# Deformable convolution in two layers: weights of two output rows side by side for the contraction

## The reference

```
value = (xf @ vp_w.T + vp_b).reshape(n, L, G, cg)           # 8 groups of 8 channels
om_in = depthwise3x3(x, dw_w) + dw_b
om    = om_in @ om_w.T + om_b                               # per pixel, group: 9 taps x (dy, dx, mask)
py, px = row + dy_tap + off_y,  col + dx_tap + off_x
sampled = bilinear gather of value at (py, px), 0 outside   # 4 neighbours
out = einsum('nhwgk,nhwgkc->nhwgc', mask, sampled) @ op_w.T
x = x + out
```

## Time and profile before

| | |
|---|---|
| median of 3 runs | 2954.0 us (2952.28 to 2957.7) |
| span of the profiled execution | 2952.3 us (its own time is not given apart) |
| TensorE, matmuls | 2707.7 us busy, 92% |
| TensorE, weight loads | 2151.1 us, 73% |
| VectorE | 2190.7 us, 74% |
| ScalarE | 2106.7 us, 71% |
| GpSimd | 1925.4 us, 65% |
| line 1273 (contraction) | 20480 matmuls, 1033.8 us busy |
| mean granted clock | 0.971 |

### The profile page before, as it was taken

One profiled execution on the slowest core, in us unless ns is written; L12 is line 12 of the kernel. 1 busy time (PEld: TensorE's weight loads), 2 busy tenths in 40 slices (PEclk: granted clock), 3 DMA queues, 4 the chain that ended last, 5 costly groups with the idle time before them and its releaser, 6 DMA issues. The chain is left out here.

```text
span 2952.3 us, 99348 instructions
## 1 busy us (share of the span) xinstructions
PE 2707.7 (92%) x40456; PEld 2151.1 (73%) x40456; DVE 2190.7 (74%) x3095; ACT 2106.7 (71%) x4273; POOL 1925.4 (65%) x1451
## 2 busy tenths in 40 slices
PE   3999789993899999999999999999999999999998
PEld 2666456772677778787778777777878787777886
DVE  3555423334989898988889797989798888989763
ACT  2444256653887878787878787787878787878782
POOL 1000000003888988888888888888988888888892
PEclk8999889996899999999999999999999999999999
DMA  4555579974677777777777786777777777777675
GB/s 106 129 127 151 131 203 265 266 192 155 163 188 198 204 202 196 191 214 194 206 194 205 186 216 186 197 204 191 208 192 214 187 205 191 205 192 213 170 182 153
DMA packets 343610, 559.00 MB, mean 189 GB/s; under 512 B 159184, under 2 KB 245712, under 8 KB 342992
## 3 DMA queue, kind: packets, MB, share of 16 engines
q1 hardware_dynamic: 284112, 461.96, 62.0%
q10 hardware_dynamic: 59136, 91.76, 8.8%
HBM read 351.36 MB, written 202.19 MB: 187 GB/s over the span
## 5 line engine op out<-in xcount | busy, mean ns | idle before, releaser
L1273 PE MATMUL acc_p<-abuf,vbd 128*32 128x170 f32 (+9 forms) x20480 | 1033.8, 371 | 10.4 <-issue 9.6
L1273 PEld LDWEIGHTS acc_p<-abuf,vbd 128*32 128x32 f32 (+1 forms) x20480 | 805.1, 144 | 230.6 <-issue 24.9
L1106 ACT ACTIVATE dwt<-xp,wts 128x224 f32<-128x224 f32 x2016 | 803.3, 487 | 41.0 <-ACT wst L1130 32.3
L977 DVE TENSOR_TENSOR pr<-mh_p,ht 128x864 f32<-128x864 f32 x672 | 668.9, 1051 | 23.2
L1250 PE MATMUL win_p<-pr,smat 128*128 128x160 f32 x4032 | 617.0, 308 | 13.2 <-POOL pr L1063 12.2
L243 PE MATMUL cv<-cin,wb 128*64 128x392 bf16 x6912 | 590.1, 333 | 26.0 <-ACT cin L222 26.0
L1250 PEld LDWEIGHTS win_p<-pr,smat 128*128 128x128 f32 x4032 | 562.6, 192 | 39.1 <-issue 13.7
L243 PEld LDWEIGHTS cv<-cin,wb 128*64 128x64 bf16 x6912 | 401.7, 110 | 208.3 <-ACT cin L222 26.1
L1046 POOL TENSOR_TENSOR dwt<-dwt 128x896 f32<-128x896 f32 x224 | 519.1, 2317 | 4.7 <-ACT dwt L1106 4.7
L1060 POOL TENSOR_TENSOR pr<-pr 128x576 f32<-128x576 f32 x224 | 316.6, 1413 | 211.4 <-DVE pr L977 211.4
L967 DVE TENSOR_TENSOR mh_p<-oms,ht 128x864 f32<-128x864 f32 x224 | 392.3, 1752 | 7.1 <-ACT ht L1121 7.1
(11 more groups left out here) (131 smaller groups left out, 2579.7 us busy)
## 6 DMA issues: line engine op xcount, KB each, us to landing
abuf<-weight_scratch SPq DMA_DIRECT2D x784, 240.0 KB, 4.1
weight_scratch<-wst ACTq DMA_DIRECT2D x112, 800.0 KB, 5.1
xt<-x SPq DMA_DIRECT2D x128, 392.0 KB, 7.5
rows_scratch<-vsb SPq DMA_DIRECT2D x224, 128.0 KB, 3.2
vbd<-rows_scratch SPq DMA_DIRECT2D x896, 32.0 KB, 4.5
x_scratch<-xt SPq DMA_DIRECT2D x64, 392.0 KB, 6.7
y<-x SPq DMA_DIRECT2D x64, 392.0 KB, 5.4
x3h<-x_scratch SPq DMA_DIRECT2D x64, 392.0 KB, 5.7
```

The lines of the kernel that those rows point to most:

```text
L977: dve.tensor_tensor(pr[:, j % 2, slots, :, :, :].rearrange("p k e x z -> p e k (x z)"), mh[:, a, :, :].rearrange("p (k x) z -> p k (x z)", ...
L1106: ins = act.activation(dwt[:, j % 2, k, :].rearrange("p (r w) -> p r w", w=W), image[:, r:r + BR, k % 3:k % 3 + W], ACT.Identity, scale=dw ...
L1273: mm = pe.matmul(acc_p[32 * (2 * s + b):32 * (2 * s + b) + 32, 0:2 * TN].rearrange("p (k w) -> p k w", w=W)[:, k0:k1 + 1, x0:x1], vbd[0:K, ...
```

## The change

The weights of two neighbouring output rows (0 and 1, 2 and 3, ...) for one value row now stand next to each other. A value row that is at distance m from the first of them is at m - 1 from the second, so the odd rows' weights are stored one distance later. That makes six distances a pixel instead of five (`RP`), 96 values instead of 80; the two places that no weight falls into stay zero (`wst` is cleared once). The order within a pixel is now distance, group, row.

The contraction reads pairs of rows, `[1, 2]` innermost, and a value row takes part for up to three pairs. The sums stand in `acc_p` as column, row of the pair, and `copy_acc` sorts them out. `copy_weights` takes four instructions, one for each row of the tile; `win_p` is laid out with 172 columns a window column for that. `copy_om` sorts the groups so that the four groups of a lane set stay together. The clamp in `hats` writes into `ht[:, u, 0]`, which the last hat then overwrites, after a wait. The bands are read back in groups of eight pixels as before, 288 KB a read.

```diff
-PC = 2 * BR * RT * 2
+RP = RT + 1
+WP = 172
+PC = 2 * BR * RP * 2
 BAND = CT * PC
-LINE = GS * 12 * PC + PC
-SEEN = 12 * PC
+PX = 8
+SEEN = (PX + CT - 1) * PC
+LINE = GS * SEEN + PC
...
-        hj = sb("hj", [LANES, 2 * TAPS, BR * G])
...
-        READS = (4, 3)
+        READS = (32 // PX, 24 // PX)
...
-                    for b in range(4 * half, 4 * half + READS[half]):
-                        m = b % 4
-                        seen = bass.AP(lines.tensor, lines.offset + 8 * b * LINE, [[SEEN, 32], [XL * LINE, S], [1, SEEN]])
-                        at = (QB * half + 8 * m) * PC
-                        sp.dma_start(abuf[32 * m:32 * m + 32, :, at:at + SEEN], seen).then_inc(a_in[half], 16)
+                    for m in range(READS[half]):
+                        seen = bass.AP(lines.tensor, lines.offset + (32 * half + PX * m) * LINE,
+                                       [[SEEN, GS * PX], [XL * LINE, S], [1, SEEN]])
+                        at = (QB * half + PX * m) * PC
+                        sp.dma_start(abuf[GS * PX * m:GS * PX * (m + 1), :, at:at + SEEN], seen).then_inc(a_in[half], 16)
...
-                        oms[:, j % 2, :, :].rearrange("q w (k g) -> q w k g", g=G),
-                        om_p[:, :].rearrange("q (k z) -> q k z", k=BR)[:, :, 0:OMC].rearrange("q k (w g) -> q w k g", g=G),
-                        ombt[:, :].rearrange("q (w g) -> q w g", g=G).unsqueeze(2).broadcast_to([LANES, 3 * TAPS, BR, G]),
+                        oms[:, j % 2, :, :].rearrange("q w (b k g) -> q (w b) k g", b=2, g=GS),
+                        om_p[:, :].rearrange("q (k z) -> q k z", k=BR)[:, :, 0:OMC].rearrange("q k (v g) -> q v k g", g=GS),
+                        ombt[:, :].rearrange("q (v g) -> q v g", g=GS).unsqueeze(2).broadcast_to([LANES, 6 * TAPS, BR, GS]),
...
+                pool.memset(wst[:, :, :], 0.0)
...
-                    act.activation(hj[:, :, :], ht[:, u, 1, :, :], ACT.Relu, bias=minus1[:, :], accum_out=far[:, bass.ts(t, 1)])
+                    act.activation(ht[:, u, 0, :, :], ht[:, u, 1, :, :], ACT.Relu, bias=minus1[:, :], accum_out=far[:, bass.ts(t, 1)]).then_inc(far_ok, 1)
                     act.activation(ht[:, u, 1, :, :], ht[:, u, 1, :, :], ACT.Identity, scale=-1.0, bias=1.0)
+                    act.wait_ge(far_ok, t + 1)
                     act.activation(ht[:, u, 0, :, :], off, ACT.Relu, scale=-1.0).then_inc(hat_ok, 1)
...
-                    for h, cells in ((0, 3), (1, 2)):
-                        m, at = RT * cells, BANK * h
+                    for k in range(BR):
+                        to = 2 * BR * (2 - 2 * (k % 2)) + BR * u + k
+                        cells = wst[:, 0, to:to + 1]
                         ins = act.activation(
-                            wst[:, :, :].rearrange("p g (m v q) -> p v m g q", v=2, q=2 * BR)[:, u, 3 * RT * h:3 * RT * h + m, :, :],
-                            win_p[:, at:at + m * BR * G].rearrange("p (m q g) -> p m g q", m=m, g=GS), ACT.Copy)
+                            bass.AP(cells.tensor, cells.offset, [cells.ap[0], [PC, CT], [2 * BR, 2 * RT], [BAND, GS]]),
+                            win_p[:, 0:CT * WP].rearrange("p (e z) -> p e z", e=CT)[:, :, 0:RT * BR * G].rearrange(
+                                "p e (m k g) -> p e m k g", k=BR, g=GS)[:, :, :, k, :],
+                            ACT.Copy)
...
-                    act.activation(accs[:, :, :].rearrange("p u f -> p (u f)"), acc_p[:, 0:2 * TN], ACT.Copy).then_inc(accs_ok, 1)
+                    act.activation(accs[:, :, :].rearrange("p u (k r w) -> p (u k) r w", r=2, w=W),
+                                   acc_p[:, 0:2 * TN].rearrange("p (t w r) -> p t r w", t=BR, r=2), ACT.Copy).then_inc(accs_ok, 1)
...
-                        k0, k1 = max(0, yq - y0 - 2), min(2 * BR - 1, yq - y0 + 2)
-                        n = k1 - k0 + 1
+                        t0, t1 = max(0, yq - y0 - 2) // 2, min(2 * BR - 1, yq - y0 + 2) // 2
...
-                                at = (QB * qb + x0 - 32 * qb + 2) * PC + 4 * BR * (y0 + k0 - yq + 2) + 2 * k0 + b
-                                mov = bass.AP(seen.tensor, seen.offset + at, [seen.ap[0], [4 * BR + 2, n], [PC, x1 - x0]])
+                                at = (QB * qb + x0 - 32 * qb + 2) * PC + 4 * BR * (y0 + 2 * t0 - yq + 3) + 2 * BR * b + 2 * t0
+                                mov = bass.AP(seen.tensor, seen.offset + at, [seen.ap[0], [8 * BR + 2, t1 - t0 + 1], [PC, x1 - x0], [1, 2]])
...
-                                    acc_p[32 * (2 * s + b):32 * (2 * s + b) + 32, 0:2 * TN].rearrange("p (k w) -> p k w", w=W)[:, k0:k1 + 1, x0:x1],
+                                    acc_p[32 * (2 * s + b):32 * (2 * s + b) + 32, 0:2 * TN].rearrange("p (t w r) -> p t w r", t=BR, r=2)[:, t0:t1 + 1, x0:x1, :],
```

More of the change, by code:

```diff
@@ L787, in l1_pass @@
         tap_ok, dw1_ok, dw2_ok, dw3_ok, dw_ok = map(sem, ("tap_ok", "dw1_ok", "dw2_ok", "dw3_ok", "dw_ok"))
-        om_ready, om_ok, abs_ok, hat_ok, mh_ok, pr_ok, mg1_ok, mg_ok = map(sem, (
-            "om_ready", "om_ok", "abs_ok", "hat_ok", "mh_ok", "pr_ok", "mg1_ok", "mg_ok"))
+        om_ready, om_ok, abs_ok, far_ok, hat_ok, mh_ok, pr_ok, mg1_ok, mg_ok = map(sem, (
+            "om_ready", "om_ok", "abs_ok", "far_ok", "hat_ok", "mh_ok", "pr_ok", "mg1_ok", "mg_ok"))
         win_ok, wst_ok, amat_ok, accs_ok, misc_ready, misc_ok, carried, passed = map(sem, (
@@ L1247, in windows @@
                         terms = [(a, b) for a in range(3) for b in range(3) if 2 - (a + b - 2) == e]
-                        to = BANK * (e // 3) + 160 * (e % 3)
+                        to = WP * e
                         for n, (a, b) in enumerate(terms):
```

## The result

Seven runs of the changed kernel have a median of 2964.5 us (2959.3 to 2966.3), beside 2953.1 for the kernel before. The ratio is 1.0034, 95% interval 1.0023 to 1.0044: a third of a per cent slower, where 2907 us were forecast. The profiled execution spans 2964.5 us, 12.2 more than the earlier trace rows.

The account below looks back on a forecast made before the run. VectorE was taken to bound each pair's first nine steps, TensorE the last five and last pair, GpSimd close behind. Gains of 13.5, 24, 3 and 6 us, together 46.5, took 2952.3 plus 1.7 to 2907; range 2850 to 2958.

Parts of the forecast that it names:

- The contraction: TensorE's matmuls on value pairs: 0.79 ns a column for 1.77, from 4.52 to 2.54 us a tile, saving 2.0.
- (b): Rival on the contraction: pairs run midway, 1.28 ns a column, 0.57 us a tile saved; 2927 us, chance 0.12.
- (c): Rival on the contraction: four streams share one reader, pace stays 1.77 ns, +0.85 us a tile; 3108 us, chance 0.05.
- rival (d): Rival on VectorE: `copy_om` slows by its upper end, 1.07 us a tile; 3041 us, chance 0.06.
- ScalarE's copy: Weight copy in four instructions of 327 to 575 ns: +0.31 to +1.30 us a tile, +0.8 taken.
- rival (a): Rival on ScalarE: its writes cost the upper end, +1.30 us a tile, nothing won in second stretch; 2937 us, chance 0.15.
- What is hidden: Clamp wait, `copy_om` and sums copy taken as 0; bands land in about 4.9 us, some 5 us slack remaining.
- The sum: Adding the gains of first stretches, second stretches, last pair and end: together 46.5 us, giving 2907.
- the second stretch: Last five steps of an image pair: TensorE falls to 35 us, stretch 47.3 to 45.7, 24 us over 15 pairs.
- The first stretch: First nine steps of a pair, VectorE busy 86.95 of 89.4 us: 0.9 us gained, 13.5 over 15 pairs.
- The end: The 72.7 us after the last pair's first nine steps: 6 us gained of up to 16.
- the shared reader: Claim of rival (c): four matmul streams share one reader, so pairs bring no faster pace; chance 0.05.

Follow-up runs that it names:

- neighbouring copies: The changed kernel with each ScalarE weight copy writing 200 neighbouring values, into wrong places: 2961.4 us, ratio 1.0041 to the kernel before.
- half the matmuls: The changed kernel without every second input row, remaining rows widened to four row pairs (same columns, half the matmuls and weight loads): 2903.6 us, ratio 0.9833.
- groups of four: Bands read in groups of four pixels for eight: in the kernel before 2949.2 us, ratio 0.9988; in the changed kernel 2925.3 us, ratio 0.9902.
- wide bands: The kernel before reading 280 KB for 240 and writing 960 for 800, added bytes unused: 2964.4 us, ratio 1.0048.

## Why the prediction was wrong, point by point

**The contraction** was right in its mechanism: 241, 307 and 359 ns, so 0.87 ns a column where 0.79 was taken; rivals (b) and (c) are out. The rule of the Trainium skill that stood beside it ("Advanced Engine Details and Errata", Memory Cachelines) agrees: two neighbouring values run at nearly full pace. The size was too good. Without a stop and at the upper clock level the two halves take 3.42 and 2.78 us (median) where they took 5.26 and 4.14, so 1.6 us a tile is saved and not 2.0, and the busy time fell to 68%, not to some 60%. Two small slips in the working, 1967 for 1961 ns and 2341 for 2329, do not bear on it, nor does the 8 us of rival (d), which comes to 7.

**ScalarE's copy** was mis-sized. Forecast were 327 to 575 ns, it is 608: +1.44 us a tile by the means, over the upper end that was to make rival (a). But (a)'s consequence fell too: the run with neighbouring copies gains nothing. TensorE, not ScalarE, is what the last five steps wait for. The rule of the Trainium skill ("Advanced Engine Details and Errata", Memory Cachelines), not confined to reads, was right on the write as well: 608 ns for single values, 334 for neighbours.

**What is hidden** is where the forecast broke. It counted the slack of the bands (5 us) and let the transfers go. The bands indeed cost little: TensorE waits for them 8.5 us in the whole run, though they land in 5.5 us, not the 4.9 forecast. The share came to 0.88, inside the 0.91 that I had bounded. What was left out is another user of the same DMA engines: TensorE's own program. The runs show its price from both sides, 118 us of stops against under 1, 61 us of time.

**The sum.** The step that failed is "TensorE falls to 35 us ... I take 45.7 for 47.3". The text named the test itself: if the second stretch keeps 47 us although the contraction falls, it is wrong there. It kept a mean of 47.9. TensorE's busy time fell to 39.6 us in the pair shown, not to 35. But that is not what holds the stretch: with half the matmuls TensorE is busy 39.2 us there, ScalarE and GpSimd work as long as here at as high a DMA share, and it takes 44.9. What differs is the stops. One of 2 us in the mean lies in the way in about every fourth tile (55 in 224), and GpSimd and ScalarE, each at 43, leave little slack to make it up. The first stretch was to gain 0.9 us and lost 1.1; I read that as stops like the one of 3.87 us above, where VectorE has only 2.5 us to spare. The end kept its 72.7 us at a DMA share of 0.72 for 0.58. Without stops the total is nearly met: half the matmuls gives 2903.6 us, beside 2907. Term by term it is not, and the agreement is partly luck: the first stretch gains 0.2 us for 0.9, the second 3.0 for 1.6 (means of 89.4 and 44.9), the end 0.5 for 6.

**The rivals.** None of the five named this; the slower side was given to the shared reader and `copy_om`, but a column takes 0.87 ns for 1.77, and `copy_om` its old 1.07 us. The hint stood in my own rows: the earlier trace rows, the lone matmul with 1.23 us of idle time "<-issue" ahead of it in the midst of a run, was read for its duration alone. It was one of the nine stops of before.

**Load and pace.** Both have a part in a late packet. The packet starts some time after the first instruction of the one before it has run: in the median 1.1 us in the kernel before with groups of four, 2.0 before, 2.9 with wide bands and 3.2 with the change, at DMA shares from 0.6 to 0.88. So it starts later at a higher load, and that the stops fall with the bytes (118, 80, 52, 23 us at 617, 560, 538, 499 MB) agrees, though the last of them has a slower run as well. With half the matmuls it starts as late, 3.1 us, but there one packet keeps TensorE for 11.2 us in the median, where it is 8.0 with the change, stops included. That 80 of 118 stay at the load of before says that the pace has the larger part.

**Still open**: how much of the 61 us is the stops themselves and how much the lower clock after them, since no run holds the clock. The clock is not likely the larger part: from 760 to 2890 us it was at the lower level for 38 us before, 201 with the change, and 177 with half the matmuls, which is the fastest but one of all these kernels.

## What to carry to other kernels

An unrolled program is itself a transfer: before making a stream of small matmuls faster, count its instructions per microsecond, and look for "issue" inside runs that hold no semaphore, with an instruction packet landing just before each ends. Where it is so, fewer and longer instructions can be worth more than fewer columns, as here, and bytes taken off the DMA queues can bring the packets sooner too. If a transfer is re-read with a margin, try the size of its groups with any change that fattens it: here four pixels for eight turned 0.3% slower into 1.0% faster, and two were too many issues.

## What was not expected of the hardware

A copy on ScalarE that writes single float32 values far apart took 608 ns for 200 values, beside 334 for neighbours: 1.37 ns a value more. TensorE restarted 1.2 to 1.6 us after the packet of its instructions had landed in 54 of 55 stops (1.9 in the other), and no packet started with more than 256 landed instructions still to run (290 before). And a stop of 3.87 us was followed by 3.4 us at 1.2 GHz.
